# Four layers of attention and experts in one launch: expert results summed by adding scatters, and smaller moves around the barriers

## The chip, the core and the metric

The kernel is one program on one core of a Trainium2 chip, written in Bass with explicit semaphores. The metric is the device time of one execution in microseconds (us). The kernel before takes 2017.86 us, the median of 3 runs (2015.39 to 2023.76). PE is TensorE, DVE VectorE, ACT ScalarE, POOL GpSimd, SP SyncE, which issues most of the transfers.

## The reference

```python
x = x + L0(_gn(x))          # x: [8, 16, 16, 256] float32, 2048 tokens of 256; _gn: group norm, 32 groups
x = x + L1(_gn(x))
t = tokens(x)
t = t + L2_attn(_ln_t(t))   # _ln_t: layer norm, no affine part
t = t + L2_ffn(_ln_t(t))
t = t + L3_attn(_ln_t(t))
t = t + L3_ffn(_ln_t(t))
```

- L0: two linear attentions without softmax (16 heads of 16), one along the columns of each image and one along its rows, summed.
- L1: softmax attention over the 256 tokens of an image, plus relative terms: `rel_h = einsum('bhwc,hkc->bhwk', q, Rh)` and the same along the width.
- L2_attn: attention over rows of the `[B*H, S, 16]` reshape (no transpose of the heads), added to its input, then a layer norm with gamma and beta.
- L2_ffn: for each token the one expert of 8 with the largest logit, `silu(x @ gate) * (x @ up) @ down`, hidden 256.
- L3_attn: ordinary softmax attention. 
- L3_ffn: `gate = x @ Wg + bias`; the 4 experts of 8 with the largest gates, softmax over those four; `out = shared(x) + sum_e w_e * swiglu_e(x)`, hidden 682.

## The kernel before

SBUF holds the tokens as `x_tokens` [128, 16 tiles, 256] for the whole run. The program is a list of stages. Each is a `Phase` with one block in which every engine has its own instruction stream, and all engines meet at its end: a barrier. The order in a stream is written out by hand. A matrix product in full precision is three products of float32r halves ("high" and "low" parts, `split_matmuls`, L85), so each operand needs a high copy and a low part by subtraction.

The stages and where they stand in the profiled span (us):

| stage | what | from, to |
|---|---|---|
| load, n0, p0, a0 | group norm, q/k/v of both linear attentions, the attentions | 0, 12.5, 31, 140 to 284 |
| n2, p2, r2, a2 | group norm, projection, relative terms, attention of layer 1 | 284, 302, 355, 412 to 612 |
| n3, p3, a3, f3 | norm, projection, attention, affine norm of layer 2 | 612, 624, 685, 907.5 to 936.7 |
| n4, g4, e4 | norm, routing, top-1 experts | 936.7, 953, 984.7 to 1107 |
| n5, p5, a5 | attention of layer 3 | 1107, 1119, 1171 to 1321 |
| n6, g6, h6 | norm, routing (top 4), shared expert | 1321, 1338, 1378 to 1528 |
| e6 | 39 packs of the routed experts, then the tail | 1528 to 1982, to 2025.4 |

`normalise` (L109) makes the statistics by VectorE unless they are there (`stats_there`), normalises, turns the tiles by TensorE, two per image, and ScalarE and VectorE evacuate them into `RT` (features in partitions). `project` (L260) runs steps of 512 tokens; queries and keys are split into three bf16 parts (`PT`, `R1`) and SP spills them to DRAM, from where the "stacks" (`Stacks` L229, `LinearStacks` L916) are loaded in the layout that attention wants, image 0 already within the projection (L256 for the rows of values, L931 for the linear stacks). `attend_linear` (L939) loads three runs ahead, queries on SP, keys on ScalarE. `relative` (L1096) clears two tables in SBUF, places 16 small blocks by DMA, multiplies them with the queries (L1157), and splits the result into three bf16 parts in eight chunks of [128, 1024]: VectorE casts twice and subtracts once (L1180), GpSimd subtracts once (L1198). `attend` (L421) handles an image in 16 units; ScalarE's exponentials stand at L764, the sums of scores at L584 and of probabilities at L606; its SP stream loads the stacks of later images, the rows of values (kind "rows", a3) and transfers the maxima (`place_max`). `affine_norm` (L2213) is f3. `route` (L1201) loads the gate matrix, makes the logits transposed (L1255), turns them back (L1260), ranks the experts by comparing all pairs (L1305), and gives each token its slot in the packs; in g6 VectorE (L1297) and GpSimd (L1363) make the low and high halves for the next stage beside it.

`shared` (h6) also scatters the rows of x by token into `scr_x4`, the packs' input in DRAM: a row is 256 values and 4 spare words, of which word 256 holds `4 * token + rank`. `streamed` (L1587) is e6: pack i of 256 rows uses one expert's weights. SP loads x (`load_x`, ring of 4), the up weights (1280 KB) and the down weights (640 KB) of each pack; up and down rings hold two. TensorE makes the hidden features in five tiles (`make_hidden`), `use_hidden` follows two tiles behind. ScalarE makes the high halves (L1749 for up), GpSimd the low ones of up, VectorE those of down and the gated product. The result of pack i is copied out of PSUM (L1795) and scattered by GpSimd in two halves of 128 rows to row `4 * token + rank` of `scr_y4` [8192, 256] (L1838). The order of SP's stream:

```python
load_x(0); load_weights(0); load_x(1); load_weights(1); load_x(2)
for i in range(2, packs):
    if i + 1 < packs: load_x(i + 1)
    load_weights(i)
```

After the last scatter the tail reads all 8192 rows back in 8 pieces; VectorE multiplies each with its gate and adds it to `x_tokens` (64 operations, L1819), and SP stores the tiles.

## Time and profile before

| | |
|---|---|
| median of 3 runs | 2017.86 us (2015.39 to 2023.76) |
| profiled execution | 2027.25 us, span 2025.4 us |
| busy, share of the span | PE 77%, PEld 60%, DVE 63%, ACT 38%, POOL 39% |
| mean granted TensorE clock | 0.873 of full speed |
| moved | 274 MB, mean 135 GB/s |

PE counts the matmuls and PEld the weight loads that overlap them. Busy shares are means over stages that have different limits; the time of one stage is read from its own stretch of the timeline. "Landing" of a transfer is the time from its issue until its semaphore is raised.

### The profile page before, as it was taken

The numbers are of one execution on the slowest core, as the hardware profiler recorded it, in microseconds if no ns is written. First come the engines' busy times: TensorE is split into PE (matmuls) and PEld (weight loads), VectorE is DVE, ScalarE is ACT, GpSimd is POOL, SyncE is SP. The second block draws the span as 40 slices with busy tenths as digits, with TensorE's granted clock in tenths as the row PEclk, the third lists the DMA queues.
The fourth block names the chain that finished last, engine by engine and source line by source line (L and its number), as shares of the span: only waits on it lengthen the run. The fifth ranks groups of instructions, "written<-read, shape, count | busy, mean of one in ns | idle before, by whom it ended". The sixth has DMA issues, their size and how long they took to land. (4 is left out here: it accounts for less than half of the span.)

```text
span 2025.4 us, 38824 instructions
## 1 busy us (share of the span) xinstructions
PE 1560.5 (77%) x13148; PEld 1210.3 (60%) x13148; DVE 1266.6 (63%) x2435; ACT 778.9 (38%) x1652; POOL 783.3 (39%) x954
## 2 busy tenths in 40 slices
PE   4957758479998486871294979938996999999990
PEld 3536644447765254551063546527886999999990
DVE  4846667656646665647224678675573777777776
ACT  2311012225452143441031246622114777777770
POOL 1431103440002510002331340015884787878770
PEclk8979889769998688895597979968997999999995
DMA  2469925353304533309222443114115666666545
GB/s 89 159 201 175 174 65 156 99 152 109 115 11 120 148 75 74 73 22 352 94 65 77 125 134 95 33 40 137 64 67 190 233 221 222 226 215 237 206 155 207
DMA packets 286765, 274.02 MB, mean 135 GB/s; under 512 B 59033, under 2 KB 263676, under 8 KB 280958
## 3 DMA queue, kind: packets, MB, share of 16 engines
q1 hardware_dynamic: 242583, 220.70, 35.7%
q10 hardware_dynamic: 35328, 29.97, 5.5%
q0 software_dynamic: 8688, 21.16, 2.9%
q8 instruction: 102, 1.67, 0.3%
q14 instruction: 64, 0.52, 0.1%
HBM read 194.74 MB, written 79.35 MB: 135 GB/s over the span
## 5 line engine op out<-in xcount | busy, mean ns | idle before, releaser
L793 DVE TENSOR_REDUCE a_maxima<-psum 128x2 f32<-128x512 f32 x384 | 257.7, 687 | 159.0 <-PE psum L584 90.8
L764 ACT ACTIVATE a_probs<-psum 128x512 f32<-128x512 f32 x384 | 224.7, 598 | 264.8 <-PE psum L606 170.7
L89 PE MATMUL psum<-e_x_split,e_up_split 128*128 128x256 f32 x2340 | 312.4, 283 | 8.3 <-DVE e_x_split L1783 8.3
L89 PEld LDWEIGHTS psum<-e_x_split,e_up_split 128*128 128x128 f32 x2340 | 293.4, 190 | 8.7 <-DVE e_x_split L1783 8.7
L1827 POOL TENSOR_TENSOR e_up_split<-e_up_raw,e_up_split 128x512 fp32r<-128x512 f32 x195 | 252.7, 1297 | 92.8 <-ACT e_up_split L1749 91.1
L1719 PE MATMUL psum<-e_down_split,e_hidden_split 128*128 128x256 f32 x1170 | 173.5, 284 | 0.4 <-DVE e_hidden_split L1809 0.4
L584 PE MATMUL psum<-s_k_stack,s_q_stack 96*128 96x256 bf16 x512 | 123.0, 295 | 41.9 <-DMA a_rel_stack<-scr_r 29.9
L1719 PEld LDWEIGHTS psum<-e_down_split,e_hidden_split 128*128 128x128 f32 x1170 | 152.4, 188 | 0.6 <-DVE e_hidden_split L1809 0.6
L1804 DVE TENSOR_TENSOR psum<-psum,e_silu 128x256 f32<-128x256 f32 x195 | 83.7, 429 | 108.6 <-ACT e_silu L1770 108.4
L1788 DVE TENSOR_TENSOR e_down_split<-e_down_raw,e_down_split 128x256 fp32r<-128x256 f32 x195 | 145.2, 745 | 0.0
L1749 ACT ACTIVATE e_up_split<-e_up_raw 128x512 fp32r<-128x512 f32 x195 | 121.4, 625 | 22.7 <-DMA e_up_raw<-in_w_ffn 22.7
L96 PE MATMUL psum<-RT,p_w_raw 128*128 128x512 f32 x256 | 118.3, 617 | 12.5 <-PEq L65 12.5
L1072 DVE TENSOR_TENSOR a_products<-psum,mask 128x512 f32<-128x512 f32 x128 | 82.8, 685 | 56.8 <-PE psum L999 56.6
L606 PE MATMUL psum<-s_q_stack,s_k_stack 98*128 98x256 bf16 x512 | 113.9, 277 | 4.4 <-DMA s_q_stack<-a_max_rows 3.3
L418 POOL TENSOR_TENSOR p_rest<-QF,p_parts 128x512 f32<-128x512 f32 x32 | 39.1, 1226 | 191.2 <-DVE p_parts L397 191.2
L889 POOL COPY a_v_image<-v 128x128 f32 (+1 forms) x64 | 18.3, 292 | 243.7 <-PE psum L640 243.5
L584 PEld LDWEIGHTS psum<-s_k_stack,s_q_stack 96*128 96x128 bf16 x512 | 45.9, 101 | 89.6 <-DMA a_rel_stack<-scr_r 30.3
L89 PE MATMUL psum<-x_split,w_split 128*128 128x512 f32 x384 | 95.2, 398 | 4.7 <-DVEq L1507 4.7
L1770 ACT ACTIVATE e_silu<-psum 128x256 f32<-128x256 f32 x195 | 75.0, 385 | 58.2 <-PE psum L89 58.2
L1775 ACT ACTIVATE e_hidden_split<-psum 128x256 fp32r<-128x256 f32 x195 | 75.1, 385 | 52.6 <-DVE psum L1804 33.0
L96 PE MATMUL psum<-a_wo_raw,a_context_t 128*128 128x256 f32 x320 | 87.4, 407 | 9.9 <-ACT a_context_t L1053 5.6
L96 PEld LDWEIGHTS psum<-RT,p_w_raw 128*128 128x128 f32 x256 | 50.4, 198 | 70.9 <-issue 70.2
(247 smaller groups left out, 3167.6 us busy)
## 6 DMA issues: line engine op xcount, KB each, us to landing
e_up_raw<-in_w_ffn SPq DMA_DIRECT2D x39, 1280.0 KB, 7.4
e_down_raw<-in_w_ffn SPq DMA_DIRECT2D x39, 640.0 KB, 4.2
s_q_stack<-scr_q SPq DMA_DIRECT2D x192, 128.0 KB, 3.2
scr_q<-p_parts SPq DMA_DIRECT2D x40, 384.0 KB, 2.7
scr_k<-p_parts SPq DMA_DIRECT2D x40, 384.0 KB, 2.9
s_k_stack<-scr_k SPq DMA_DIRECT2D x114, 128.0 KB, 2.8
scr_x<-empty_row ACTq DMA_DIRECT2D x1, 10140.0 KB, 48.1
e_x_pack<-scr_x SPq DMA_DIRECT2D x39, 260.0 KB, 4.8
```

What stands on the lines that cost most here:

```text
L89: last = eng.matmul(out, lhs(a, k), rhs(b, k), start=i == 0, stop=i == len(terms) - 1)
L96: last = eng.matmul(out, lhs(k), rhs(k), start=k == 0, stop=k == n_k - 1)
L584: last = pe.matmul(s_bank(u)[:, t, :], cols(QS, STACK, slot, u, t, P), cols(KS, STACK, slot, u, 0, SEQ), start=True, stop=not rel)
L606: last = pe.matmul(st_bank(u)[:, t, :], cols(KS, K, slot, u, t, P), cols(QS, K, slot, u, 0, SEQ), start=True, stop=not rel)
L764: act.activation(PB[:, u % PR], st_bank(u), ACT.Exp, scale=0.25).then_inc(S["probs"], 1)
L793: dve.tensor_reduce(MX[:, u // 8, :, u % 8], s_bank(u), AX.X, ALU.max).then_inc(S["s_used"], 1)
L1072: dve.tensor_tensor(PB[:, 2 * p:2 * p + 2], st_bank(p), masks[:].unsqueeze(1).to_broadcast([P, 2, 2, P]), ALU.mult).then_inc(S["masked"], 1)
L1719: last = pe.matmul(out_bank(i, t), GS[:, a, c % 2, t * P:(t + 1) * P], down(i % 2, b, m), start=m == 0 and n == 0, stop=m == n_h - 1 and n ...
L1749: act.activation(tile_of(SU[:, r, 0], m), tile_of(RU[:, r], m), ACT.Copy).then_inc(S["up_hi"], 1)
L1788: dve.tensor_tensor(SD[:, r, 1, q], RD[:, r, q], SD[:, r, 0, q], ALU.subtract).then_inc(S["down_lo"], 1)
L1804: dve.tensor_tensor(hidden, ps[:, c % 2, PACK4:2 * PACK4], SL[:, c % 2], ALU.mult).then_inc(S["hidden"], 1)
L1827: pool.tensor_tensor(tile_of(SU[:, r, 1], m), tile_of(RU[:, r], m), tile_of(SU[:, r, 0], m), ALU.subtract).then_inc(S["up_lo"], 1)
```

## The change

Nothing of the arithmetic of the reference is changed; sums of the routed experts are made in another place and order. In the order of the program:

1. `project`, p0: the 36 loads of the linear stacks start at step 2 instead of the third last, two behind each spill. `attend_linear`: SP loads the six query parts and two of the key parts, ScalarE four key parts one half-run later than it issued six before, for the run three ahead.
2. A class `Tables` clears the relative tables on GpSimd and loads them on SP at the start of p2. `relative` works in eight units of half the tokens, writes the float result and the first bf16 part on ScalarE, keeps its intermediates in `RT` and `KF`, and loads the relative stack of image 0 (a2 did that).
3. p3: the value rows of image 0 are loaded by ScalarE in the last two steps instead of by SP behind the third; a value spill waits for the one before. a3: the value rows of image i+2 are issued by ScalarE, two per unit in units 8 to 15, instead of by SP at the end of a step; it also makes the statistics for f3, and adds beta to `x_tokens` on GpSimd at its end. a5 makes the statistics for n6.
4. `affine_norm` has no statistics and no beta; GpSimd centres and scales 3 of the 16 tiles; the transfers ahead are issued behind the square root.
5. `normalise` of n4 and n6 loads the gate matrix and makes the logits, tokens in partitions, between the transposes. `route` begins at the copy of the logits; comparisons are bf16; in g6 ScalarE makes the high half of x and GpSimd, behind its weights, the low half (VectorE did both); the softmax gates come before the slots.
6. Rows of x carry the gate (word 257) and the token as an integer (word 258). `streamed` multiplies by the gate while it copies out of PSUM, and both scatters of pack i-1 go behind up tile 3 of pack i, each adding to the row of its token in a table `scr_y4` of [2304, 256]. The table is seeded with `x_tokens` and, for 256 spare rows to which empty slots point, with zeros. At the end one DMA copies 2048 rows from DRAM to `out`. The x ring has 5 places.

The core of the diff:

```diff
 class Tables, project (p2), relative (r2)
+    def clear(self, eng):
+        for axis in range(2):
+            eng.memset(self.T[:, axis].rearrange("p q m -> p (q m)"), 0.0).then_inc(self.zeroed, 1)
+    def load(self, eng, rel):
+        eng.wait_ge(self.zeroed, 2)
+        for axis, table in enumerate(rel):
+            for j in range(8):
+                rows = slice(j * DH, (j + 1) * DH)
+                eng.dma_start(self.T[rows, axis, :, rows], table).then_inc(self.placed[axis], 16)
...
+                        act.activation(in_order(F[:, c % SLOTS, :], c, g), bank(c, g), ACT.Copy, scale=4.0).then_inc(ready, 1)
+                        act.activation(in_order(PT[:, c % SLOTS, 0, :], c, g), bank(c, g), ACT.Copy,
+                                       scale=4.0).then_inc(part1, 1)
-                dve.tensor_copy(PT[:, c % SLOTS, 0], rel_half(c)).then_inc(part1, 1)
...
 project (p0), attend_linear (a0)
-                    if linear is not None and n == STEPS - 3:
+                    if linear is not None and n == 2:
                         for u in range(4):
                             sp.wait_ge(spilled[u], 32)
...
+                        first = 4 * (n - 2) + u
+                        if linear is not None and 0 <= first < linear.RING * len(PAIRS):
+                            b, i = divmod(first, len(PAIRS))
+                            for j in range(2):
+                                linear.load(sp, jobs[0][3 + j], b, b, j, i)
...
 attend (a3), ScalarE
+                        if rows and more and u >= 8:
+                            if u == 8:
+                                act.wait_ge(S["v_copied"], index(i, 4, 4))
+                                act.wait_ge(S["v_loaded"], index(i, 256, 512))
+                            stacks.load_v(act, scr_v, i + 2, range(2 * (u - 8), 2 * (u - 8) + 2))
...
 normalise (n4, n6), TensorE
+                def logits(b):
+                    pe.wait_ge(evacuated, b + 1)
+                    for t in (2 * b, 2 * b + 1):
+                        last = matmuls(pe, ps[:, 4, t * ROUTED:(t + 1) * ROUTED], lambda k: RT[:, k, t * P:(t + 1) * P],
+                                       lambda k: WG[:, k, :], KD)
+                    last.then_inc(logits_done, 1)
...
 route (g6)
-                    dve.tensor_copy(XS[:, 0], RT[:]).then_inc(x_hi, 1)
-                    dve.tensor_tensor(XS[:, 1], RT[:], XS[:, 0], ALU.subtract).then_inc(x_lo, 1)
+                    act.activation(G["x_split"][:, 0], RT[:], ACT.Copy).then_inc(x_hi, 1)
+                    pool.tensor_tensor(XS[:, 1], RT[:], XS[:, 0], ALU.subtract).then_inc(x_lo, 1)
...
 streamed (e6)
-    LAG, RINGX = 2, 4
+    LAG, RINGX = 2, 5
...
                 def load_x(i):
                     if i >= RINGX:
                         sp.wait_ge(S["x_turned"], i - RINGX + 1)
-                        sp.wait_ge(S["id_ready"], HALVES * (i - RINGX + 1))
+                        sp.wait_ge(y_stored[(i - RINGX) % 2], 16 * HALVES * ((i - RINGX) // 2 + 1))
...
+                sp.dma_start(scr_y[0:TOKENS, :].rearrange("(t p) d -> p t d", p=P), X[:]).then_inc(S["seeded"], 16)
...
-                for c in range(TILES // CHUNK):
+                sums = scr_y[0:TOKENS, :].rearrange("(p r) d -> p (r d)", p=P)
+                rows = out.rearrange("b y x c -> (b y x) c").rearrange("(p r) d -> p (r d)", p=P)
+                sp.dma_start(rows, sums).then_inc(S["stored"], 16)
...
-                    dve.tensor_copy(Y[:, i % 2], banks).then_inc(S["y_ready"], 1)
+                    dve.tensor_tensor(Y[:, i % 2], banks, gates.to_broadcast([P, HALVES, D]),
+                                      ALU.mult).then_inc(S["y_ready"], 1)
...
+                def scatter(i):
                     pool.wait_ge(x_loaded[i % RINGX], 16 * (i // RINGX + 1))
+                    pool.wait_ge(S["y_ready"], i + 1)
+                    if i:
+                        pool.wait_ge(y_stored[(i - 1) % 2], 16 * HALVES * ((i - 1) // 2 + 1))
+                    else:
+                        pool.wait_ge(S["seeded"], 32)
+                    for j in range(HALVES):
+                        ids = XT[:, i % RINGX, j, TOKEN:TOKEN + 1].bitcast(mybir.dt.uint32)
+                        pool.indirect_dma_start(scr_y, bass.IndirectOffsetOnAxis(ap=ids, axis=0), Y[:, i % 2, j, :], None,
+                                                bounds_check=TOKENS + PACK4 - 1,
+                                                compute_op=ALU.add).then_inc(y_stored[i % 2], 16)
```

## Rows read from the trace of the kernel before

**Rows 1.** windows: start:end, length, each engine's busy time (count), clock, DMA share, GB/s.

```profile
935.00:945.00 10.00, 0.00 (x0) 0.00 (x0) 8.56 (x41) 0.22 (x1) 0.00 (x0) 0.50 1.08 338
...
1528.00:1982.00 454.00, 438.13 (x3666) 437.32 (x3666) 325.78 (x663) 329.12 (x819) 347.11 (x351) 0.98 0.60 212
...
1982.00:2025.40 43.40, 0.00 (x0) 0.00 (x0) 29.70 (x64) 0.00 (x0) 0.69 (x1) 0.50 0.66 242
```

**Rows 2.** chain of waits: when a step begins, how long it lasts, what it is.

```profile
1983.84 4.81 DMA e_y_back<-scr_y
```

**Rows 3.** issues of 1540 to 1982, median us to landing; L1838's scatters: landing.

```profile
e_up_raw<-in_w_ffn SPq DMA_DIRECT2D x37, 1280.0 KB, 7.2
...
DMA to landing us min/median/max: 2.1/5.3/7.8
```

**Rows 4.** timeline in e6: start, busy time, engine, line, what, [idle before, releaser].

```profile
1711.16 0.38 SPq L1657 DMA_DIRECT2D e_x_pack<-scr_x  x1
...
1712.95 0.99 POOL L1838 DMA_INDIRECT scr_y<-e_y_pack,e_row_of_slot  x1 [0.17 <-issue]
...
1712.96 0.34 SPq L1647 DMA_DIRECT2D e_up_raw<-in_w_ffn  x1
...
1723.64 0.62 ACT L1749 ACTIVATE e_up_split<-e_up_raw 128x512 fp32r<-128x512 f32 x1
```

**Rows 5.** timeline of r2 and the start of a2.

```profile
365.41 23.26 PE L1157 MATMUL psum<-u_tokens,r_tables 128*128 128x128 f32 x128 [18.18 <-DMA r_tables<-in_rel_h]
...
388.43 2.51 POOL L1198 TENSOR_TENSOR r_rest<-r_rel,r_parts 128x1024 f32<-128x1024 f32 x1 [1.76 <-DVE r_parts L1186]
...
388.99 3.04 DVE L1180 TENSOR_TENSOR r_parts<-r_rest,r_parts 128x1024 bf16<-128x1024 f32 x1
...
418.61 0.40 PE L584 MATMUL psum<-s_k_stack,s_q_stack 96*128 96x256 bf16 x1 [29.93 <-DMA a_rel_stack<-scr_r]
```

**Rows 6.** timeline at the end of p0; a0's waits: sum, times, longest.

```profile
98.47 1.97 SPq L931 DMA_DIRECT2D s_q_stack<-scr_q  x3
...
140.30 2.72 PE L999 MATMUL psum<-s_q_stack,s_k_stack 96*128 96x128 bf16 x24 [21.91 <-PEq L65]
...
PE psum L999 <- DMA s_k_stack<-scr_k: 13.4, 7, 2.9
```

**Rows 7.** timeline of p3 and a3, SP's value loads and ScalarE's exponentials.

```profile
668.49 7.95 SPq L256 DMA_DIRECT2D s_v_rows<-scr_v  x16
...
747.53 9.69 SPq L256 DMA_DIRECT2D s_v_rows<-scr_v  x16
...
767.25 0.60 ACT L764 ACTIVATE a_probs<-psum 128x512 f32<-128x512 f32 x1 [6.21 <-PE psum L606]
...
849.57 0.60 ACT L764 ACTIVATE a_probs<-psum 128x512 f32<-128x512 f32 x1 [7.44 <-PE psum L606]
...
870.91 0.60 ACT L764 ACTIVATE a_probs<-psum 128x512 f32<-128x512 f32 x1 [0.39 <-PE psum L606]
```

**Rows 8.** timeline of f3.

```profile
907.60 5.33 DVE L2242 BATCH_NORM_STATS2 stats<-u_tokens 128x6 f32<-128x256 f32 x16 [2.21 <-PEq L65]
...
914.66 13.42 DVE L2251 SCALAR_TENSOR_TENSOR u_tokens<-u_tokens,f_mean_var,f_gamma_beta 128x256 f32<-128x256 f32 x16 [0.46 <-DMA f_gamma_beta<-in_L_attn_beta]
```

**Rows 9.** timeline of g4.

```profile
958.22 9.55 PE L1255 MATMUL psum<-x_norm,g_wg 128*8 128x512 f32 x16 [6.97 <-DMA g_wg<-in_L_ffn_Wg]
...
969.64 0.29 DVE L1301 COPY g_logits<-psum 128x128 f32<-128x128 f32 x1 [19.65 <-PE psum L1260]
```

**Rows 10.** timeline of n6 and g6.

```profile
1328.98 3.41 ACT L180 ACTIVATE w_split<-w_raw 128x3840 fp32r<-128x3840 f32 x1 [0.96 <-DMA w_raw<-in_w_ffn]
...
1338.17 8.27 POOL L1363 TENSOR_TENSOR w_split<-w_raw,w_split 128x3840 fp32r<-128x3840 f32 x1 [37.60 <-POOLq L65]
...
1338.18 10.40 DVE L1297 CAST x_split<-RT 128x4096 fp32r<-128x4096 f32 x1 [3.74 <-PEq L65]
...
1353.60 1.23 DVE L1305 TENSOR_TENSOR g_compared<-g_logits 128x1024 f32<-128x1024 f32 x1
```

403 lines of the change are left out of this document (194 added, 209 removed).

## The prediction

> **What bounds the kernel now.** I read the timeline of the page first, then the busy time by stage, then inside each touched stage the timeline rows and the waits. The reader is to see that no single engine bounds the program. It is a chain of stages with a barrier between each two. The last but one, the stream of routed expert packs, holds 454 us with TensorE busy for 438.13; the tail behind it holds 43.4 us in which TensorE does nothing, and VectorE only adds 64 slices [rows 1]. The change leaves TensorE's products in that stream alone. It edits the starts, ends and gaps of the stages, so the sum is made stage by stage. I call the stages p0 and a0 (projection and attention of layer 0), p2, r2, a2 (layer 1 and its relative tables), p3, a3 (layer 2), f3, n4, g4 (affine norm, norm, routing), n6, g6, h6, e6 (norm, routing, shared expert, packs).
>
> **The sum, part by part.** It stands against the profiled execution: 2027.25 us, span 2025.4, so 1.85 around it. The median shown, 2017.86, lies 9.4 below.
>
> *Tail.* From the first read-back at 1983.84 [rows 2] to the end of the span are 41.6 us: 8 MB of rows read back, 64 additions, stores. After, the last scatter adds into the table, and one copy of 2.1 MB goes from DRAM to DRAM. No such copy is in the trace. Lower bound: 2.1 MB at the 338 GB/s of a fill [rows 1], 6.2 us, plus 2.1 us, the shortest landing [rows 3]. Upper bound: twice the transfer, because each byte is also read, 14.5. I take 10.5, plus 2 for the later landing of an adding scatter and 1 for the end: 13.5. Gain 28 (23 to 33).
>
> *e6, the stream.* Removed: two small casts per pack on GpSimd; added: a gate product in place of a copy on VectorE, same size. Neither is on TensorE's path. What matters is a new wait. The rows of x carry gate and token until the scatter has used them, so SP's load of pack i+4 waits until the scatter of pack i-1 has landed. Behind it in SP's queue stand the up weights of pack i+3. Now SP issues x at 1711.16 and up at 1712.96 [rows 4]; the second scatter goes at 1712.95 and would go 1.2 earlier, both being issued after the same subtraction: 1711.75. If it lands after L, up is issued at 1711.75 + L + 1.8 and lands 7.2 later [rows 3], at 1720.75 + L. ScalarE wants it at 1723.64 [rows 4]. TensorE runs about one unit of hidden features ahead of ScalarE (a fifth of a pack of 11.1 us); so I give 2.5 us more. Free up to L = 5.4. Beyond that, one us of L costs half a us per pack, as the loop spans two packs: 18.5 us over 37 packs. A plain scatter lands in 2.1 / 5.3 / 7.8 [rows 3], the median beside the up transfer that would now not be in flight. The addition needs a read before the write, at most another 2.1. So L lies between 2.1 and 9.9: cost 0 to 83. I take 5.7, near the median: +5. The seed of the table (2.4 MB, before pack 2's weights) has 12 us of cover while packs 0 and 1 run: 0, at most +3.
>
> *r2 and a2's start.* Clearing and loading the tables goes into p2. TensorE's first matmul of r2 waits for them until 365.41 [rows 5], 9 us after the stage began. Each of the eight chunks costs 4.27 us now: casts of 0.6 twice, GpSimd's subtraction, and VectorE's, which takes 3.04 beside it [rows 5]. One cast goes to ScalarE: 8 x 0.6 = 4.8. Matmuls are twice as many at half the columns; 256 records at 0.1 us are 26, under the chunks' 29; at the lower granted clock (1.2 GHz) they would be the bound, +4. Gain 13 (8 to 18). a2's first matmul waits for the relative stack until 418.61 [rows 5], 6.4 after the stage began; now loaded during r2: gain 6. In p2, 16 table transfers of 0.65 us stand on SP before the first spill: +1.5 (0 to 4), which the spills' slack does not hide as the buffers are single.
>
> *p0 and a0.* In p0's last three steps SP issues three stack loads of 0.65 us behind each spill [rows 6], and the steps take 14.4 us where the others take 9.6. Spread over five steps with two each I work out 11.9 for four steps and 10.5 for one: equal in sum (+0.4), but the last step has no loads left behind it: 6 less before a0 starts. Gain 6 (2 to 9). In a0 the key loads come half a run earlier, and ScalarE issues four, not six, ahead of its copies. TensorE's waits for keys are 13.4 us [rows 6]. The engines of the DMA are near full there, so half: gain 7 (0 to 12).
>
> *p3 and a3.* 16 value loads stand in SP's queue before p3's last spills, 7.95 us [rows 7]; VectorE had its last step ready 5 us before they went. Now ScalarE issues them: gain 5. In a3 SP issues 16 value loads in 9.69 us per image, and the maxima's transfer behind them makes ScalarE wait 6.21 us in the middle of each image [rows 7]. Without it a period is 21.3 us, as the last but one shows (849.57 to 870.91); with it about 27.2. But the 16 issues now stand on ScalarE, in the second half of each image: 8 x (0.6 + 1.3) + 1 = 16.2 us where that half took 12.4. Period 25. Step 0, which had no stall in its second half, loses 5. Sum over the stage: gain 7 (-2 to 12; at the worst the issues fill no idle time). The statistics added to a3 and a5 (0.8 us of VectorE per image) hide in its waits for TensorE: 0 and +1. The additions of beta run on GpSimd beside the last image of a3.
>
> *f3.* 16 statistics go, 5.33; the scaling of 16 tiles takes 13.42 beside GpSimd's additions [rows 8], 13 tiles without these about 8. Gain 9.6 (7 to 12).
>
> *n4 and g4.* The product with the gate matrix waits 6.97 us for its weights, starts at 958.22, is copied, turned and reaches VectorE at 969.64 [rows 9]. Now 8 x 8 weight loads of 128 columns go between n4's transposes, whose own pace is 0.7 us per image: 5.7 becomes 12.5 (11 to 16), then VectorE starts. Gain 9.7 (5 to 11).
>
> *n6 and g6.* The statistics gone from n6 gain nothing: ScalarE first splits the weights, from 1328.98 on [rows 10], and evacuates only then. With the logits between the transposes, n6 ends near 1344.5 and g6 starts at 1345.7. In g6 the low half of x is subtracted by GpSimd, 4096 columns against the 3840 that take 8.27 [rows 10], so 8.8. The row beside it shows what this does: a VectorE cast that needs about 2 us took 10.40. If comparisons wait likewise, they start 17.3 us after g6's start instead of at 1353.60 [rows 10]; the rest of the chain takes 16, two less than now; the next stage starts 3.4 us later than before: +3.4. If they do not, 16 are gained.
> The Trainium skill (SBUF — State Buffer, "Who interferes with whom") says that a VectorE instruction with two SBUF inputs and a GpSimd instruction that reads SBUF exclude each other for the whole instruction, while a VectorE reduction is free of it. By that rule the comparisons wait; the sum would be 16 us better without it. The rows show it for a cast and for a subtraction [rows 5, 10], not for a comparison of broadcast operands.
>
> Sum: -28 +5 -13 -6 +1.5 -6 -7 -5 -7 +1 -9.6 -9.7 +3.4 = -90.4. Own time 1937; against the median 2017.86: **1928 us**.
>
> **Rivals.**
> A: the adding scatter is slower than I take it, L from 6.4 to 9.4. SP's wait then holds up the weights of two packs on. For: the plain maximum is 7.8 already. Against: the competing transfer moves behind it. At L = 7.7, +43 instead of +5: 1966.
> B, the slower side: the same loop with L = 11.5. Cost (11.5 - 5.4) x 18.5 = 113, sum +18: 2036. It decides from L = 10.3, where the loop eats all 90. Against: it needs an addition costing more than twice the median of a plain scatter.
> C: the sum is too careful: g6's comparisons run beside GpSimd (-16), or a0 and a3 give their full 12 each (-10): 1912.
> D: that the change does not do what it says, the tail's read-back merely replaced: a DRAM to DRAM copy of 30 us. Its price of 20 lies inside the main case's range.
>
> **How the numbers follow.** Main case 0.56 (own range 1908 to 1948, the independent bounds above added as squares), A 0.22, C 0.13, B 0.09. The range 1903 to 1988 leaves out B and the ends of A and C. A measurement of this kernel tells about 0.5% (10 us) from no change. Faster takes main, A's nearly whole and C: 0.89; same 0.02; slower 0.09.
>
> **What would show it.** Tail: one DMA out, under 15 us, no VectorE behind the last pack. e6: period still 11.1 and TensorE busy above 96%; wrong if SP's weight issues slide after the scatter's landing and ScalarE waits for up weights in each pack. r2: TensorE starts at once, chunk period 3.7. a3: no 6 us gap in mid image, but gaps of 1.3 between exponentials in the second half. g6: the first comparison starts as GpSimd's second subtraction ends. n4: TensorE last in the stage. The prediction is wrong if e6 grows by over 20 us, or if the stages ahead of e6 together give less than 35.

## The result, and the profile after

The changed kernel takes 2050.83 us (median of 4 runs, 2047.46 to 2058.68) against 2017.82 us of the kernel before beside it: a ratio of 1.0177, 95% interval 1.015 to 1.0204. It is slower by 1.8% (1.5 to 2.0), and 1928 us with a range of 1903 to 1988 was forecast. The profiled execution has a span of 2045.6 us, 20.2 above that of before.

First the page's busy line, then two stretches by windows (length, busy time and count of PE, PEld, DVE, ACT, POOL, granted clock, DMA share, GB/s): the packs of e6, and the tail. They answer to [rows 1].

```profile
PE 1588.2 (78%) x13340; PEld 1255.5 (61%) x13340; DVE 1332.9 (65%) x2359; ACT 783.5 (38%) x1613; POOL 816.1 (40%) x886
...
1509.00:2026.00 517.00, 447.12 (x3666) 438.78 (x3666) 448.61 (x663) 313.01 (x819) 367.23 (x271) 0.98 0.68 193
...
2026.00:2045.60 19.60, 0.00 (x0) 0.00 (x0) 0.40 (x1) 0.00 (x0) 3.35 (x3) 0.60 0.48 128
```

The tail shrank from 43.4 to 19.6 us, but the packs take 517 us where they took 454, and TensorE, which was busy for 438.13 of 454, is now idle for 70 of 517 us. Stage by stage, from the first instruction of a stage to that of the next (us):

| stage | before | after | change | forecast |
|---|---|---|---|---|
| p0 and a0 | 254.1 | 233.1 | -21.0 | -13 |
| p2 | 52.9 | 54.0 | +1.1 | +1.5 |
| r2 | 55.86 | 67.49 | +11.6 | -13 |
| a2 | 200.39 | 192.58 | -7.8 | -6 |
| n3 and p3 | 73.1 | 65.1 | -8.0 | -5 |
| a3 | 221.90 | 208.83 | -13.1 | -7 |
| f3 | 29.16 | 38.12 | +9.0 | -9.6 |
| n4 and g4 | 48.0 | 44.7 | -3.3 | -9.7 |
| a5 | 149.36 | 151.32 | +2.0 | +1 |
| n6 and g6 | 57.0 | 67.8 | +10.8 | +3.4 |
| packs of e6 | 454 | 517 | +63 | +5 |
| tail | 43.4 | 19.6 | -23.8 | -28 |

The stages that are not listed change by under 1 us each. So the stages ahead of e6 gave 18 us together, not the 57 that the prediction's terms for them add up to, and the packs cost 58 us more than forecast.

What a pack looks like now. The timeline of one period of e6 (start, busy time, engine, line, what, idle time before and what ended it):

```profile
1662.26 1.56 POOL L1862 DMA_INDIRECT scr_y<-e_y_pack,e_x_pack  x1 [0.16 <-issue]
...
1664.13 1.55 POOL L1862 DMA_INDIRECT scr_y<-e_y_pack,e_x_pack  x1 [0.30 <-issue]
...
1664.84 4.91 DVE L1817 TENSOR_TENSOR e_down_split<-e_down_raw,e_down_split 128x256 fp32r<-128x256 f32 x1
1665.03 0.39 ACT L1804 ACTIVATE e_hidden_split<-psum 128x256 fp32r<-128x256 f32 x1 [0.26 <-PE psum L1748]
1665.14 4.32 POOL L1851 TENSOR_TENSOR e_up_split<-e_up_raw,e_up_split 128x512 fp32r<-128x512 f32 x3
...
1668.47 0.38 SPq L1696 DMA_DIRECT2D e_x_pack<-scr_x  x1
1669.61 0.34 SPq L1686 DMA_DIRECT2D e_up_raw<-in_w_ffn  x1
1669.68 0.41 DVE L1841 TENSOR_TENSOR e_hidden_split<-psum,e_hidden_split 128x256 fp32r<-128x256 f32 x1
...
1670.14 0.97 PE L1748 MATMUL psum<-e_down_split,e_hidden_split 128*128 128x256 f32 x6 [1.67 <-DVE e_hidden_split L1841]
```

The reader is to see four things. The two adding scatters stand one behind the other on GpSimd, 1662.26 and 1664.13, and take 1.56 and 1.55 us where one took 0.99 [rows 4]. Behind them GpSimd works off three up subtractions without a gap, 4.32 us. VectorE's down subtraction, which takes 0.41 elsewhere, is recorded from 1664.84 to 1669.75, its waiting included: it ends 0.3 us after GpSimd's row of three is over. TensorE then has waited 1.67 us for the hidden features that VectorE makes behind it. The fourth is what hardly happens: a wait for the up weights.

The groups of lines in 1600 to 1950 (count, then busy us, mean ns and idle time before): the two subtractions and ScalarE's first touch of the up weights.

```profile
L1817 DVE TENSOR_TENSOR e_down_split<-e_down_raw,e_down_split 128x256 fp32r<-128x256 f32 x134 | 192.0, 1433 | 0.0
L1851 POOL TENSOR_TENSOR e_up_split<-e_up_raw,e_up_split 128x512 fp32r<-128x512 f32 x135 | 186.7, 1623 | 83.0 <-ACT e_up_split L1778 83.0
...
L1778 ACT ACTIVATE e_up_split<-e_up_raw 128x512 fp32r<-128x512 f32 x134 | 83.7, 624 | 2.0 <-DMA e_up_raw<-in_w_ffn 1.8
```

And the landing of the adding scatters, from the view of their one line:

```profile
DMA to landing us min/median/max: 3.8/4.9/5.5
```

Their median, 4.9 us, is below the plain ones' 5.3 [rows 3]: the quantity that the prediction turned on, L, was 0.8 below what was taken. ScalarE waits for up weights 1.8 us in 350. Two rows of the waits in 1600 to 1900 (us in total, times, longest) set the forecast mechanism beside the measured one:

```profile
SPq L1694 <- DMA scr_y<-e_y_pack,e_x_pack: 128.3, 23, 6.5
...
PE psum L1748 <- DVE e_hidden_split L1841: 38.2, 23, 1.7
```

SP does stand waiting for the landing of a scatter in every pack, as forecast, but the weights behind it still come in time. All of TensorE's waiting in these 300 us is for VectorE's hidden features, 1.66 us in each pack.

**r2.** A window and the timeline of the relative stage after:

```profile
336.00:404.00 68.00, 54.84 (x256) 54.69 (x256) 15.36 (x16) 34.41 (x32) 17.07 (x9) 0.50 0.30 105
...
354.68 2.38 ACT L1233 ACTIVATE r_parts<-psum 128x512 bf16<-128x512 f32 x1
```

The trace has 256 matmul records of 64 columns, each with a weight load. They are busy for 54.8 of 68 us at a granted clock of 0.50, that is 1.2 GHz: 0.214 us each, twice the 0.1 that was taken. ScalarE's second output takes 2.38 us where the layout is strided, and 0.59 in the other half of the units. Three windows of r2 in the kernel before, with 128 columns in a record, show what such a record cost there:

```profile
365.41:369.40 3.99, 3.99 (x18) 3.99 (x19) 0.00 (x0) 0.95 (x5) 0.00 (x0) 0.50 0.26 25
369.40:375.00 5.60, 5.60 (x51) 5.58 (x50) 1.29 (x2) 4.80 (x26) 2.22 (x1) 1.00 0.04 4
376.00:388.00 12.00, 12.00 (x57) 11.35 (x56) 11.89 (x9) 5.31 (x23) 6.40 (x3) 1.00 0.36 133
```

That is 0.21 us at 1.2 GHz and 0.11 at 2.4 GHz, and 0.21 again at 2.4 GHz in the second half of the stage, where the queries are read with a stride of 16 elements. There the clock rose 4.0 us after the first matmul. In the changed kernel it stays at 1.2 GHz to the end of r2, though TensorE is busy without a break for more than 50 us.

**f3.** Timeline of its end and of the next stage's start:

```profile
881.75 6.42 DVE L2291 SCALAR_TENSOR_TENSOR x_tokens<-u_tokens,f_rstd,x_tokens 128x256 f32<-128x256 f32 x16
883.32 24.24 ACTq L2270 DMA_DIRECT2D scr_x<-empty_row  x2
...
908.63 3.69 DVE L222 BATCH_NORM_STATS2 stats<-x_tokens 128x6 f32<-128x256 f32 x11 [20.46 <-PEq L66]
```

VectorE is done 17.7 us after the stage's start, as forecast. But ScalarE's issue of the second half of the fill lasts 23.75 us (the row counts the issues of both halves), and the barrier waits for it. Before, the fill was one transfer, issued at 919.38 in 0.46 us.

**n4 and g6.** TensorE's logits of one image and the next image's transposes in n4; in g6 GpSimd's second subtraction and VectorE's first comparison:

```profile
921.02 1.09 PE L181 MATMUL psum<-ident,x_rows 128*128 128x128 f32 x4
921.90 1.72 PE L97 MATMUL psum<-n_wg,x_norm 128*128 128x8 f32 x8
923.47 1.09 PE L181 MATMUL psum<-ident,x_rows 128*128 128x128 f32 x4
...
1331.33 8.85 POOL L1405 TENSOR_TENSOR x_split<-RT,x_split 128x4096 fp32r<-128x4096 f32 x1
1331.56 9.71 DVE L1338 TENSOR_TENSOR g_compared<-g_logits 128x1024 bf16<-128x1024 f32 x1
```

An image now takes 2.45 us of TensorE in n4 and n6, where the prediction's 12.5 us for eight images is 1.56 each; before, without the logits, it took 0.71 and 0.79. The comparison waits for GpSimd as forecast: its record ends 18.1 us after g6's start, 1.1 after GpSimd's.

**Tail.** The issue and landing of the copy out:

```profile
out<-scr_y SPq DMA_DIRECT2D x1, 8.2
```

8.2 us for 2.1 MB from DRAM to DRAM; 10.5 was taken.

### The profile page after: what moved, and what is told of

Same layout as the page of the kernel before. It is cut to its first block and busy times, and to the rows that moved or that the text cites. A ratio compares the mean times of both kernels' runs of the same rounds, so it can differ in the third digit from the quotient of the medians.

```text
span 2045.6 us, 38966 instructions
## 1 busy us (share of the span) xinstructions
PE 1588.2 (78%) x13340; PEld 1255.5 (61%) x13340; DVE 1332.9 (65%) x2359; ACT 783.5 (38%) x1613; POOL 816.1 (40%) x886
## 3 DMA queue, kind: packets, MB, share of 16 engines
q0 software_dynamic: 16176, 22.99, 5.4%
## 5 line engine op out<-in xcount | busy, mean ns | idle before, releaser
L1851 POOL TENSOR_TENSOR e_up_split<-e_up_raw,e_up_split 128x512 fp32r<-128x512 f32 x195 | 268.7, 1600 | 134.4 <-ACT e_up_split L1778 134.4
L1817 DVE TENSOR_TENSOR e_down_split<-e_down_raw,e_down_split 128x256 fp32r<-128x256 f32 x195 | 266.8, 1368 | 0.0
L1748 PE MATMUL psum<-e_down_split,e_hidden_split 128*128 128x256 f32 x1170 | 178.9, 288 | 58.0 <-DVE e_hidden_split L1841 58.0
L1862 POOL DMA_INDIRECT scr_y<-e_y_pack,e_x_pack x78 | 121.8, 1562 | 24.5 <-issue 16.9
L97 PE MATMUL psum<-a_wo_raw,a_context_t 128*128 128x256 f32 x320 | 90.4, 418 | 5.1 <-ACT a_context_t L777 4.6
```

The lines of the kernel that those rows point to most:

```text
L97: last = eng.matmul(out, lhs(k), rhs(k), start=k == 0, stop=k == n_k - 1)
L1748: last = pe.matmul(out_bank(i, t), GS[:, a, c % 2, t * P:(t + 1) * P], down(i % 2, b, m), start=m == 0 and n == 0, stop=m == n_h - 1 and n ...
L1817: dve.tensor_tensor(SD[:, r, 1, q], RD[:, r, q], SD[:, r, 0, q], ALU.subtract).then_inc(S["down_lo"], 1)
L1851: pool.tensor_tensor(tile_of(SU[:, r, 1], m), tile_of(RU[:, r], m), tile_of(SU[:, r, 0], m), ALU.subtract).then_inc(S["up_lo"], 1)
L1862: pool.indirect_dma_start(scr_y, bass.IndirectOffsetOnAxis(ap=ids, axis=0), Y[:, i % 2, j, :], None, bounds_check=TOKENS + PACK4 - 1, comp ...
```

## The experiments

The first theory, T: GpSimd's subtractions pile up behind its scatters, and while they run in a row VectorE cannot start a subtraction with two inputs in SBUF. "Lockout" below is short for that. The rivals: R1, SP's wait for the landing, the prediction's own mechanism; R2, the adding scatter's longer issue; R3, its traffic; and, later, T2, that GpSimd is simply late with the up halves. "Period" is the mean spacing of SP's loads of x between 1600 and 1900 us: 11.14 before, 13.02 after. Except for e1, e8, e11, e12, e15 and e17 each version was executed once; the executions of the kernel before that are compared here range from 2006.0 to 2023.8 us, so the argument goes by the periods and by the waits in the traces more than by the times.

**e1_spread.**

```diff
-                        if m == LAG + 1 and i:
-                            scatter(i - 1)
+                        if i and m >= n_h - HALVES:
+                            scatter(i - 1, (m - n_h + HALVES,))
```

> The changed kernel with one edit: the two adding scatters of a pack are issued one after up tile 3 and one after up tile 4 of the next pack, as the kernel before places its plain ones, not both after tile 3. Theory T (lockout): two scatters in a row hold GpSimd for 3.4 us, three up subtractions pile up behind them and run without a gap for 4.3 us, and VectorE's down subtraction, which has two SBUF inputs, cannot start beside them (4.9 us where it needs 0.42). Spread, at most two pile up: period of a pack 11.2 to 11.7 us instead of 13.0, the time 1985 to 2000. Rival R1 (SP's wait for the scatter's landing holds up the weights): nothing changes, period 13.0, 2050. Rival R2 (an adding scatter simply takes 1.56 us of GpSimd instead of 1.0, wherever it stands): period 12.5 or more, 2030 or more.

Measured: 2049.62 us, ratio to before 1.0157 (1.013 to 1.0184), period 12.98. T's number failed. The timeline shows why it need not fall:

```profile
1664.18 1.56 POOL L1863 DMA_INDIRECT scr_y<-e_y_pack,e_x_pack  x1
...
1665.09 2.27 DVE L1817 TENSOR_TENSOR e_down_split<-e_down_raw,e_down_split 128x256 fp32r<-128x256 f32 x1
...
1665.25 1.82 POOL L1851 TENSOR_TENSOR e_up_split<-e_up_raw,e_up_split 128x512 fp32r<-128x512 f32 x1
...
1667.23 1.56 POOL L1863 DMA_INDIRECT scr_y<-e_y_pack,e_x_pack  x1 [0.17 <-issue]
...
1668.25 3.38 DVE L1817 TENSOR_TENSOR e_down_split<-e_down_raw,e_down_split 128x256 fp32r<-128x256 f32 x1
1668.29 3.05 POOL L1851 TENSOR_TENSOR e_up_split<-e_up_raw,e_up_split 128x512 fp32r<-128x512 f32 x2
```

One lockout of 4.9 us has become two, of 2.3 and 3.4. A scatter of 1.56 plus a subtraction of 1.30 is more than a tile's 2.14, so spreading over neighbouring tiles doubles the occasions. So R1 and R2 were still standing after this run.

**e2_plain_pair** and **e3_before_pair.**

```diff
 e2, in the changed kernel
-                                                bounds_check=TOKENS + PACK4 - 1,
-                                                compute_op=ALU.add).then_inc(y_stored[i % 2], 16)
+                                                bounds_check=TOKENS + PACK4 - 1,
+                                                oob_is_err=False).then_inc(y_stored[i % 2], 16)
 e3, in the kernel before
-                        if i and m >= n_h - HALVES:
-                            scatter(i - 1, m - n_h + HALVES)
+                        if i and m == LAG + 1:
+                            for j in range(HALVES):
+                                scatter(i - 1, j)
```

> The changed kernel with plain scatters instead of adding ones, still both after up tile 3 (the sums over a token's experts are left out: the last one written stays). T: GpSimd is held 2.3 us instead of 3.4; two or three subtractions still pile up, the down subtraction behind them takes 2 to 4 us instead of 4.9: period 11.7 to 12.5. R2 (the addition is the cause): period 11.1, the time 1975. R3 (the read of the addition contends with the weight loads): 11.1 too, and the up weights land in 7.2 us as before.

> The kernel before with one edit: its two plain scatters of a pack both after up tile 3. T: a pile-up and lockout appear here too, though there is no addition and no wait for a landing: period 11.7 to 12.5 instead of 11.14, the time 2040 to 2070. R1 and R2: unchanged, 2018.

Measured: e2 2005.8 us, period 11.76; e3 2045.17 us, period 11.92. In e3 nothing is new but the place of one plain scatter, and it costs 0.78 us per pack, 27 us in all. Its timeline holds the same picture:

```profile
1664.05 1.02 POOL L1838 DMA_INDIRECT scr_y<-e_y_pack,e_row_of_slot  x1 [0.15 <-issue]
...
1665.37 0.97 POOL L1838 DMA_INDIRECT scr_y<-e_y_pack,e_row_of_slot  x1 [0.30 <-issue]
...
1666.35 3.79 POOL L1827 TENSOR_TENSOR e_up_split<-e_up_raw,e_up_split 128x512 fp32r<-128x512 f32 x3
1666.63 3.80 DVE L1788 TENSOR_TENSOR e_down_split<-e_down_raw,e_down_split 128x256 fp32r<-128x256 f32 x1
...
1670.82 0.99 PE L1719 MATMUL psum<-e_down_split,e_hidden_split 128*128 128x256 f32 x6 [0.51 <-DVE e_hidden_split L1809]
```

So R1 and R3 are not needed for this part, and R2 is not the whole: in e2 the plain scatters in a row cost 0.6 us per pack, and the addition 1.3 more. It also takes 1.15 us more of GpSimd per pack; that this, and not its traffic, makes the 1.3 is settled only by e16.

**e4_spread_wide.**

```diff
+                        if m == LAG + 1 and i:
+                            scatter(i - 1, (0,))
+                        if m == 0 and i >= 2:
+                            scatter(i - 2, (1,))
```

> The changed kernel with the two scatters three tiles apart (after up tile 3, and after tile 0 of the pack behind), and a ring of 6 for x so that the later landing holds nothing up. T: only one subtraction waits behind a scatter, never two: period 11.14, TensorE busy throughout, the time 1980. If it is no faster than the version with one tile between them, the pile-up there is harmless already. R1: with the wider ring and the later scatter the wait is about as it was, 13.0.

Measured: 2020.28 us, period 12.23, between T's 11.14 and R1's 13.0. Two tiles between the scatters help, but the first still makes a pair of subtractions run in a row, once in each pack (3.06 us, VectorE's subtraction 3.52).

**e9_spread6** (e1 with `LAG, RINGX = 2, 6`).

> The spread version (scatters after tiles 3 and 4) with a ring of 6 for x in place of 5: SP's load of x waits for the scatter of a pack one earlier. In the spread version ScalarE waits 0.37 us per pack for the up weights. R1 (SP's wait matters there): period 12.5 or less instead of 13.0, the time 2030 or less. T (only the pile-ups count): the wait for the weights goes, the lockout of 3.4 us and that of 2.3 us stay, period 12.7 to 13.0, 2037 to 2050.

Measured: 2042.42 us, period 12.99 against 12.98. The waits between 1600 and 1900 us (us in total, times, longest): e1 has this row of ScalarE for up weights, and e9 has none:

```profile
ACT e_up_split L1778 <- DMA e_up_raw<-in_w_ffn: 7.9, 12, 1.7
```

R1 is excluded as the cause: its wait went, and the period stayed.

**e13_turn_pair** and **e14_turn_spread.** One wait is added to the changed kernel (e13), and to e9 (e14):

```diff
                         if i + 1 < packs:
+                            pool.wait_ge(S["down_lo"], i * n_h + m + 1)
                             low_up(i + 1, m)
```

> The changed kernel with one wait added, nothing else: before GpSimd subtracts an up tile of the next pack it waits until VectorE has done the down subtraction of the same step. Where nothing is late that has been done already; after the two scatters it makes GpSimd let VectorE go first, so no down subtraction stands behind more than one of GpSimd's. Theory T (the cost is the time in which VectorE is shut out by a row of GpSimd subtractions): the 4.9 us falls to at most 1.8, the period from 13.03 to 11.3 to 11.9 us, the time 1985 to 2010. Rival T2 (TensorE waits because GpSimd's up halves come late after 3.4 us of scatters, and the lockout is only its companion): an added wait makes GpSimd later still, period 13.0 or more, 2050 or more.

> The same wait in the version with the scatters after tiles 3 and 4 and a ring of 6 for x (which without it took 12.9 us per pack). T: period 11.15 to 11.5, TensorE busy over 96%, the time 1975 to 1990. T2: 12.9 or more.

Measured: e13 2015.94 us, period 12.39; e14 2025.37 us, period 12.30. In e13 a wait more on the engine that is late makes stage e6 25 us shorter (535.9 to 510.9); the run as a whole is 35 us faster, and the rest lies in stages that the edit does not touch. ScalarE waits 13.0 us in 300 for up weights there. T2 forecast the opposite sign and falls. T's numbers were too good. In e13, shown below, VectorE makes two down subtractions while the scatters run, so two of GpSimd's are free to go at once and hold the next one of VectorE for 2.7 to 3.7 us. In e14 no two run in a row, but the one behind each scatter holds VectorE for 2.3 us, twice in a pack.

```profile
1713.15 1.55 POOL L1862 DMA_INDIRECT scr_y<-e_y_pack,e_x_pack  x1 [0.30 <-issue]
...
1713.86 3.69 DVE L1817 TENSOR_TENSOR e_down_split<-e_down_raw,e_down_split 128x256 fp32r<-128x256 f32 x1
...
1714.17 3.09 POOL L1851 TENSOR_TENSOR e_up_split<-e_up_raw,e_up_split 128x512 fp32r<-128x512 f32 x2
...
1717.63 1.28 POOL L1851 TENSOR_TENSOR e_up_split<-e_up_raw,e_up_split 128x512 fp32r<-128x512 f32 x1 [0.37 <-DVE e_down_split L1817]
```

**e16_no_lockout.**

```diff
 ScalarE, high_down
                     act.activation(SD[:, r, 0, q], RD[:, r, q], ACT.Copy).then_inc(S["down_hi"], 1)
+                    act.activation(SD[:, r, 1, q], RD[:, r, q], ACT.Copy).then_inc(S["down_lo"], 1)
 VectorE
-                        low_down(i, m)
```

> The changed kernel, both scatters after tile 3, but VectorE's down subtraction is left out: ScalarE writes a plain copy in its place (the low half of the down weights is wrong, the shapes and the number of products stay). VectorE then has no instruction with two SBUF inputs in the loop. T (the lockout is the whole cost): GpSimd's row of three subtractions after its scatters remains, but nobody waits for it; period 11.15 to 11.5 us (ScalarE has 2.1 us more of work per pack, 10.5 of 11.15), the time 1975 to 1990. T2 (GpSimd's late up halves): 13.0, 2045.

Measured: 1982.61 us, period 11.24, within T's 11.15 to 11.5. GpSimd's row is still there, in most packs of three and in some of four, and TensorE waits 1.2 us in 300:

```profile
1717.00 1.56 POOL L1862 DMA_INDIRECT scr_y<-e_y_pack,e_x_pack  x1 [0.16 <-issue]
...
1718.87 1.55 POOL L1862 DMA_INDIRECT scr_y<-e_y_pack,e_x_pack  x1 [0.30 <-issue]
...
1719.88 5.63 POOL L1851 TENSOR_TENSOR e_up_split<-e_up_raw,e_up_split 128x512 fp32r<-128x512 f32 x4
1720.50 0.43 DVE L1837 TENSOR_TENSOR psum<-psum,e_silu 128x256 f32<-128x256 f32 x1 [1.73 <-ACT e_silu L1800]
...
1721.38 0.42 DVE L1841 TENSOR_TENSOR e_hidden_split<-psum,e_hidden_split 128x256 fp32r<-128x256 f32 x1 [0.45 <-ACT e_hidden_split L1805]
```

Here four of GpSimd's subtractions run in a row for 5.63 us, and VectorE's two operations with an operand in PSUM take their usual 0.43 and 0.42 beside them. Of the 1.88 us per pack 1.78 go with the one instruction that had two inputs in SBUF. The edit also takes 5 times 0.41 us of work from VectorE; but the kernel before has that work too, at 11.14, so it alone is not the cause, and e13, which takes none away, points the same way. e16 keeps the addition, its traffic and SP's wait for the landing: what R1, R2 and R3 cost without the lockout is therefore 0.10 us per pack, unless VectorE's lighter load hides more, though ScalarE waits for up weights 31.5 us in 300 here.

**e8_share** and **e10_share4.** VectorE makes one of the five up tiles: tile 3, with the scatters after tiles 3 and 4 (e8); tile 4, with the scatters after tile 3 and tile 0 (e10).

```diff
 VectorE, e8
+                        if m == BY_DVE + 1 and i + 1 < packs:
+                            low_up(i + 1)
 VectorE, e10
+                        if m == 0 and i:
+                            low_up(i)
 GpSimd
-                        if i + 1 < packs:
+                        if i + 1 < packs and m != BY_DVE:
                             low_up(i + 1, m)
```

> The changed kernel with VectorE making the low half of up tile 3 (one of five per pack), the scatters after the places of tiles 3 and 4, a ring of 6 for x. Theory T (GpSimd's subtractions pile up behind a scatter and shut VectorE out): GpSimd has 4 x 1.30 + 2 x 1.56 = 8.3 us per pack instead of 9.6, the pile-ups shrink to one or none, period 11.2 to 11.5 us, the time 1985. Rival (VectorE's own load is the bound now): its 7.7 us plus 0.7 and what waits of it make the period 12 or more, 2015 or more.

> The changed kernel with VectorE making the low half of up tile 4, in the pack's own tile 0, and GpSimd's two scatters after up tile 3 and after up tile 0 of the pack behind, a ring of 6 for x. T: no two subtractions of GpSimd stand behind one scatter, so no down subtraction of VectorE takes over 1.5 us: period 11.15 to 11.4 us, TensorE busy over 97%, the time 1985 to 1998. Rival: VectorE's load bounds it: period 11.6 as with tile 3 shared, 2011.

Measured: e8 2011.18 us, ratio to before 0.9984 (0.9965 to 1.0002), period 11.91; e10 2007.22 us, period 12.25. Both are better than the changed kernel. By the length of stage e6 alone e8 is the better of the two (494.8 us against 502.2; 535.9 in the changed kernel). Neither is as good as T said, e10 by 0.9 us per pack: I had not seen that the second scatter after tile 0 leaves tiles 1 and 2 in a row (GpSimd 3.07 us, VectorE's subtraction 3.03).

**e5_late_fill, e6_rel_old, e7_logits_back** each undo one of the small stages.

```diff
 e5: the second half of the fill, at the start of e4 on ScalarE
+                dst, src, landed = G["late"]
+                act.dma_start(dst, src).then_inc(landed, 16)
                 copy_x(0)
 e6: relative as before, the tables still from p2
-        UNITS = [(half, axis, t) for half in range(2) for axis in range(2) for t in range(KD)]
+        UNITS = [(axis, t) for axis in range(2) for t in range(KD)]
 e7: route as before, the gate matrix loaded by normalise
-                normalise(nc, rows, "n4", "layer", wg=A["L2_ffn_Wg"])
+                normalise(nc, rows, "n4", "layer", [(G["WG"][:], A["L2_ffn_Wg"])])
```

> The changed kernel with the second of the two halves of the x4 fill issued by ScalarE at the start of e4, not in f3. In f3 VectorE is done 17.7 us after the stage began, but the stage takes 38.1 us: ScalarE's issue of the second half lasts 23.75 us. Theory: a second transfer of this size behind the first in one queue blocks the issuing engine until room comes free; moved to a time when the first has landed it is issued in under 1 us. f3 falls from 38.1 to 18 to 20, n4 and g4 stay, e4 grows by 0 to 5; the time 2030 to 2035. Rival: the fills' bandwidth holds the stage, and the time comes back in n4 or e4, for the 5 MB move anyway: 2045 to 2050.

> The changed kernel with the products and splits of `relative` as the kernel before had them (128 matmuls of 128 columns, casts of the first part on VectorE), the tables still loaded in p2, the relative stack of image 0 loaded at the stage's end. Theory: a matmul of this stage costs what its weight load of 128 columns costs, 0.214 us at the lower clock, whatever its columns, so half the columns doubled TensorE's time (23.3 to 54.8 us): r2 falls from 67.5 to 44 to 50 us, the time 2030. Rival: ScalarE's second output (2.4 us where the columns are strided) and the spills set the stage, and TensorE only waits: r2 stays above 58.

> The changed kernel with the logits made in route by 8 products of 512 columns against the gate matrix as weights, turned back by 16 transposes, as before; the gate matrix is loaded during the norm. Theory: 64 weight loads of 128 columns at 0.214 us between the transposes are 13.7 us of TensorE in each norm; n4 falls from 30.5 to 17, g4 rises from 14.2 to 26 to 28 (the sum 44.7 becomes 43 to 45); in g6 the comparisons wait for GpSimd until 18 us after the start anyway, so the products hide there: n6 31.9 to 17 to 18, g6 stays at 36 to 37, the sum 67.8 becomes 54. The time 2035. Rival: the comparisons of g6 wait for the logits, not for GpSimd: g6 grows to over 45 and the sum stays over 62.

Measured: e5 2032.71 us, f3 38.1 to 18.6, e4 +1.1; e6 2035.2 us, r2 67.5 to 51.6; e7 2028.61 us, n4 and g4 44.7 to 40.4, n6 and g6 67.8 to 54.0. Each is near what was expected: r2 is a little above it, n4 and g4 are 3 us below it. Issue rows of the fills in e5:

```profile
886.78 0.46 ACTq L2274 DMA_DIRECT2D scr_x<-empty_row  x1
...
936.48 0.38 ACTq L1995 DMA_DIRECT2D scr_x<-empty_row  x1
```

**e11_all, e12_old_stream, e15_all_turns, e17_share_turns** put the three mended stages together with four streams: e10's, that of the kernel before with its tail, e14's, and e10's with the wait of e13.

> The shared version of e10 with the late fill, the products of `relative` as before, and the logits back in route. The stages add, so from e10's time 18 (f3), 16 (r2) and 18 (n4 to g6) go: 1985 to 1998 less 52 is 1933 to 1946 us, against 2018 of the kernel before. Rival: part of it comes back elsewhere (the fill beside e4, the clock): 1955 to 1965.

> All of e11 except the stream: scatters of 4 x 2048 rows without addition, ids as floats, the read-back and the 64 additions at the end as in the kernel before. Theory: against e11 the tail is 23 us longer and a pack 0.05 to 0.3 us shorter (2 to 12 us): 1945 to 1960. So the adding scatter is worth 10 to 20 us once its place costs nothing. Rival: the longer issues of adding scatters (1.56 us against 1.0) cost the stream as much as the tail gives: e12 equals e11 within 5 us.

> The turn-taking and spread stream with the late fill, the products of `relative` as before, and the logits back in route. T: 1975 to 1990 less 52: 1923 to 1938 us, 20 to 35 below the version with the old stream (1961). T2: the stream costs what it costs in the changed kernel, 1985 or more.

> The stream of e10 (VectorE makes up tile 4, scatters after tile 3 and tile 0) with the turn-taking wait of e13, and the three small stages mended as in e11. In e11 two of GpSimd's subtractions still ran in a row and held a down subtraction for 3.0 us per pack. T: with turns at most 1.8 us; period from 12.2 to 11.5 to 11.9: 12 to 27 us off e11's 1966, 1939 to 1954. Rival: the waits in turn only move the delay, as e15 showed against e11: 1960 to 1970.

| kernel | us | ratio to before | 95% interval | period |
|---|---|---|---|---|
| e11_all | 1965.66 | 0.9765 | 0.9739 to 0.9791 | 12.25 |
| e12_old_stream | 1960.75 | 0.9727 | 0.9706 to 0.9747 | 11.13 |
| e15_all_turns | 1968.79 | 0.9769 | 0.9751 to 0.9787 | 12.28 |
| e17_share_turns | 1937.30 | 0.9613 | 0.9587 to 0.9639 | 11.23 |

The stages add as expected: all ahead of e6 take 1509.6 us in the changed kernel and 1456.5 to 1461.7 in e11, e15 and e17, that is 48 to 53 less, where 52 was taken. The misses of e11 and e15 (1933 to 1946 and 1923 to 1938 were forecast) are those of their streams. e17 came out a little better than forecast. With its stream the adding scatters, and VectorE's share of the subtractions with them, are worth 23 us (e17 against e12); with a period of 12.25 they were worth nothing, as e12's rival said (e12 is 4.9 us below e11). e17's packs by windows (columns as above):

```profile
1451.00:1916.00 465.00, 440.05 (x3678) 432.29 (x3678) 388.65 (x706) 313.98 (x819) 327.25 (x237) 0.97 0.71 216
```

And a lockout in them, from the timeline of e17:

```profile
1704.33 1.82 POOL L1885 TENSOR_TENSOR e_up_split<-e_up_raw,e_up_split 128x512 fp32r<-128x512 f32 x1
...
1704.59 1.85 DVE L1842 TENSOR_TENSOR e_down_split<-e_down_raw,e_down_split 128x256 fp32r<-128x256 f32 x1
...
1706.52 1.30 POOL L1885 TENSOR_TENSOR e_up_split<-e_up_raw,e_up_split 128x512 fp32r<-128x512 f32 x1 [0.37 <-DVE e_down_split L1842]
```

VectorE's subtraction is held for 1.85 us here and 2.28 us at most in the packs; GpSimd's next subtraction goes behind it, and TensorE's matmuls fill 440 of 465 us. One thing stays open: one such hold in a pack costs e17 0.1 us against the kernel before, two of 2.3 us cost e14 1.2. GpSimd also has less to do in e17 (8.3 us of subtractions and scatters in a pack, 9.6 in e14), and no run separates the two. e17 is the fastest version: 3.9% below the kernel before, 5.5% below the changed one.

## Why the prediction was wrong

The terms of the prediction's sum add to -80.4, not to -90.4: by its own terms the forecast was 1937 us, and rivals A and B would have stood at 1975 and 2045. This slip moves no sign, and 1937 misses too. Between -80.4 and the +20.2 of the profiled executions lie 101 us: 58 in e6, 25 in r2, 19 in f3, 14 in n4 to g4 and n6 to g6 together, and 4 in the tail, against 19 that p0 and a0, a3, p3 and a2 gave beyond the forecast.

**e6, the step that failed.** The prediction said of the edits to GpSimd and VectorE "Neither is on TensorE's path. What matters is a new wait", and put the whole cost of the stream on SP's wait for the landing of the adding scatter. SP does wait there, but it cost the period nothing (e9), and the landing was 4.9, not 5.7. What it passed over is the moved second scatter: it said "the second scatter goes at 1712.95 and would go 1.2 earlier" and took from that only when the scatter lands, not what is queued behind it on GpSimd. e3 prices the move by itself at 0.78 us per pack, an adding scatter in place of a plain one makes it 1.88, and e16 shows that the path is the lockout of VectorE's down subtraction. Its own working had the mechanism at hand: [rows 5, 10] show a VectorE subtraction of 1024 columns that took 3.04 us beside GpSimd, where a comparison of as many took 1.23, and a cast that took 10.40; I used it for g6 alone. The same rows stood in e6 of before, where a down subtraction takes 0.77 us in the mean for 0.41. Rivals A and B had the right place and about the right size of loss (e6 at +43 and at +113, measured +63) with the wrong cause; their condition, L from 6.4 on, was not met. That B's time comes near the measured one is luck.

By the rule of the Trainium skill that the prediction weighed for g6 (SBUF — State Buffer, "Who interferes with whom"), a VectorE instruction with two SBUF inputs and a GpSimd one that reads SBUF take turns, and VectorE's operations with at most one SBUF input, outside its two-port modes, are free. The traces agree in g6 (9.71 us for a comparison of 1.2) and in e6: 4.91 for 0.41 with two, 0.43 as ever with one (e16). The measurement adds that a row of three of GpSimd's instructions lets VectorE in at no gap (4.91 us beside a row of 4.32).

**The adding scatter's issue.** The prediction gave the addition a later landing and no cost on GpSimd; it takes 1.56 us of GpSimd where a plain one takes 1.00, and the page counts 16176 packets in the software queue instead of 8688. The Trainium skill (Collectives: The Full Stack, "Why ReduceScatter is half of AllGather") says of the reduce step that an addition in a transfer needs two read descriptors per chunk where a copy needs one. The count here grows by more than that: with plain scatters in the same places (e2) it is 8688 again, so each of the 78 adding scatters brings 96 packets more, on about 48 (an estimate, 8688 over the queue's 181 scatters). No run here shows the descriptors themselves.

**r2, n4, n6: one mis-sized term.** "256 records at 0.1 us are 26" is the price of the better half of the stage at 2.4 GHz. The stage ran at 1.2 GHz throughout, at 0.214 us each, 54.8, and TensorE became the bound. The prediction named this case and gave it +4; twice its own 26 is 52, 23 above the chunks' 29. [rows 5] held a warning: 23.26 us for 128 records are 0.18 each, a mean over both clocks and both halves. Half the columns did not make a record cheaper at 1.2 GHz (0.21 for 128, 64 and 8 columns), and with 64 columns the clock did not rise. Whether it stays down because of them, no run separates; in the run e6_rel_old, with 128 columns again, it rises 4.1 us after the first matmul. The same price was under n4's 12.5 us, which measured 19.6 (64 records more, 13.7 us), and under n6's. The runs e6 and e7 undo this and give 16 and 18 us back in these stages.

**f3.** The arithmetic was right (VectorE done after 17.7 us; 9.6 gained was the forecast, and e5 gains 10.6 against before). What failed is that this step priced ScalarE's issues at nothing: two transfers of 5 MB in one queue are not one of 10. It cost 19.5 us in the stage, of which e5 gets 18 back in all.

**Right or better.** a2 (-7.8 for -6), p2 (+1.1), p3 (-8.0 for -5), a5 (+2.0), the wait of g6's comparisons, and the tail (-23.8 for -28: the copy was 2.3 us cheaper than taken, but the last scatters wait one for the other, 3.0 us, and take 1.56 each). p0 gained 1.4 instead of 6. a0 gained 19.5 instead of 7: TensorE's waits for keys of [rows 6] are gone, and its same 1664 matmuls are busy for 101.7 us instead of 112.0, at a mean granted clock of 0.94 instead of 0.88, for which the prediction had no term. a3 gained 13.1 instead of 7: the period of its middle images is 24.6 us in the mean (27.2 before, 25 forecast), and the 5 us that step 0 was to lose were not lost (20.9 us, 20.8 before).

The rivals C and D played no part. The bounds were too narrow because the sum had no term for an engine that is made late and shuts out another, nor for the issues of f3, and too small a one for the lower clock in r2.

## What to carry to other kernels

Before moving work on GpSimd, list what is queued behind it, and count how many instructions that read SBUF will then run in a row: in these traces a VectorE subtraction with two SBUF inputs waited for the whole row (3.0 us for two, 3.8 to 4.9 for three), and a wait that gave VectorE its turn was a gain. Price small matmuls by the record, at the clock that the stage is granted, and not by their columns. Two large transfers in one queue can hold the engine that issues the second; an issue that a barrier waits for belongs where the queue is empty.

## What the runs showed of the hardware that was not expected

- An adding scatter of 128 rows of 256 floats takes 1.56 us of GpSimd, a plain one 1.00; it lands as fast (median 4.9 us; plain ones 5.3 in the kernel before, 4.7 in the same places in e2).
- A row of GpSimd subtractions without a gap holds a VectorE subtraction with two SBUF inputs to its end: 4.91 us for 0.41 beside three after adding scatters, 3.80 beside three after plain ones (e3). An added wait on GpSimd shortened stage e6 by 25 us (e13).
- A 5 MB fill issued behind another on one queue held ScalarE for 23.75 us; in e5, issued 49.7 us after the first, it took 0.38 us, and one of 10 MB took 0.46 (before). In stage e6, SP's second seed transfer, 256 rows behind 2048, held SP for 10.5 us.
- A DRAM to DRAM copy of 2.1 MB landed in 8.2 us.
- A float32 matmul record with new weights of 128 columns takes 0.21 us at 1.2 GHz, with 128 columns (r2 before), 64 (r2 after) or 8 (n4 after) alike. At 2.4 GHz it took 0.11 with 128 columns, and 0.21 where these were read with a stride of 16 elements (r2 before); no run changes the stride alone.
- The granted clock stayed at 1.2 GHz through r2's 54.8 us of matmuls of 64 columns; with 128 columns it rose 4.0 us after the first (before).
